# Routing inside the attentions: rows scattered to their experts, results scattered to token order, plain loads elsewhere

## What is computed

```python
logits = flat @ gate_w + gate_b                      # flat: layernorm of x, [4096, 128]
topv, topi = lax.top_k(logits, TOP_K)                # TOP_K = 2 of E = 8
topw = jax.nn.softmax(topv.astype(jnp.float32), axis=-1).astype(x.dtype)
routing = jnp.zeros_like(logits).at[jnp.arange(T)[:, None], topi].set(topw)
def body(acc, params):
    W1e, b1e, W2e, b2e, we = params
    h = jax.nn.gelu(flat @ W1e + b1e, approximate=False)
    out = h @ W2e + b2e
    return (acc + out * we[:, None], None)
...
x = x + attention_a(layernorm(x));  x = x + experts(layernorm(x))
x = x + attention_b(layernorm(x));  x = x + experts(layernorm(x))
```

## Time and profile before

| | |
|---|---|
| median of 3 runs | 1292.41 us (1289.14 to 1292.47) |
| the profiled execution, its own time | 1287.89 us |
| its span, first to last instruction | 1284.0 us |
| busy share of the span | PE 83%, DVE 63%, ACT 51%, POOL 67% |
| mean granted clock of TensorE | 0.898 of full speed |

### The profile page before, as it was taken

How to read it: one execution, slowest core, us unless ns; L and a number is a source line. 1 busy time by engine, 2 the same in 40 slices (tenths; PEclk the granted TensorE clock), 3 DMA queues, 4 the chain that set the end, 5 groups by cost and what they waited for, 6 DMA issues and landing times.

```text
span 1284.0 us, 31775 instructions
## 1 busy us (share of the span) xinstructions
PE 1068.1 (83%) x11367; PEld 807.3 (63%) x11368; DVE 811.3 (63%) x2010; ACT 650.4 (51%) x1205; POOL 865.6 (67%) x1161
## 2 busy tenths in 40 slices
PE   4699999999999757999978799999998488999200
PEld 3466676677666445999944466666665358999200
DVE  5788787788776384556426767777664754655222
ACT  1376676676766301555514567777774104555000
POOL 0599989989988256555154789998762375553576
PEclk8799999999999957999986899999998678999655
DMA  5400000000000101223310000000000002333232
GB/s 115 113 22 2 10 3 10 11 2 10 10 3 10 34 0 38 76 74 79 57 33 13 22 14 24 24 26 18 2 10 18 26 22 65 79 75 63 58 85 71
DMA packets 56248, 45.73 MB, mean 36 GB/s; under 512 B 13570, under 2 KB 48258, under 8 KB 56130
## 3 DMA queue, kind: packets, MB, share of 16 engines
q0 software_dynamic: 9088, 18.63, 6.5%
q1 hardware_dynamic: 43490, 22.46, 6.4%
q10 hardware_dynamic: 3552, 3.02, 0.9%
HBM read 27.57 MB, written 16.52 MB: 34 GB/s over the span
## 4 chain that ended last, share of the span: by engine, by line
PE 60%; DVE 13%; POOL 10%; issue 9%; ACT 4%; DMA 2%; another core or an unknown queue 2%; SPq 1%; DVEq 0%; ACTq 0%; POOLq 0%
PE PS L1778 11%; PE PS L1445 6%; PE PS L1514 5%; PE PS L1447 5%; PE PS L1565 5%; PE PS L1446 5%; POOL got L677 5%; PE PS L1496 3%; PE PS L1503 2%; PE PS L1545 2%; POOL PT L575 2%; DVE M L900 2%; PE PS L1485 1%; PE PS L1580 1%
## 5 line engine op out<-in xcount | busy, mean ns | idle before, releaser
L575 POOL TENSOR_SCALAR_AFFINE_SELECT PT<-PT 128x256 f32<-128x256 f32 x512 | 221.5, 457 | 82.4 <-ACT PT L1223 80.6
L1223 ACT ACTIVATE PT<-PS 128x768 f32<-128x768 f32 x256 | 207.1, 809 | 100.2 <-PE PS L1683 50.7
L706 POOL DMA_INDIRECT xg<-normed,source x156 | 150.9, 967 | 115.3 <-PE PS L1756 78.3
L677 POOL DMA_INDIRECT got<-expert_rows,slot_of x128 | 122.3, 956 | 79.0 <-DMA expert_rows<-y_rows 46.3
L1358 ACT ACTIVATE hid<-PS,b_cols 128x256 f32<-128x256 f32 x312 | 122.5, 476 | 102.9 <-PE PS L1447 80.0
L1778 PE MATMUL PS<-W,hid 128*128 x1248 | 155.2, 278 | 2.8 <-issue 1.8
L1778 PEld LDWEIGHTS PS<-W,hid 128*128 128x128 f32 x1248 | 148.7, 195 | 4.1 <-issue 4.1
L1514 PE MATMUL PS<-PT,v_aug 128*32 128x256 f32 (+1 forms) x2048 | 113.6, 341 | 5.4 <-POOL PT L575 5.3
L1496 PE MATMUL PS<-causal_b,ident_b 128*128 128x256 bf16 x512 | 101.9, 283 | 8.3 <-DVE q_aug L976 8.3
L1177 DVE SCALAR_TENSOR_TENSOR X<-got,weight,X 128x128 f32<-128x128 f32 x128 | 51.9, 406 | 81.1 <-DMA got<-expert_rows,slot_of 75.4
L1445 PE MATMUL PS<-xg_hi,w_hi 128*128 128x256 f32 x312 | 94.9, 304 | 3.7 <-issue 3.7
(11 more groups left out here) (264 smaller groups left out, 3227.3 us busy)
## 6 DMA issues: line engine op xcount, KB each, us to landing
expert_rows<-y_rows SPq DMA_DIRECT2D x78, 128.0 KB
normed<-xn SPq DMA_DIRECT2D x16, 256.0 KB, 2.3
xg<-normed,source POOLq DMA_INDIRECT x156
W<-in_L_ffn_w_dram SPq DMA_DIRECT2D x1, 2048.0 KB, 10.3
got<-expert_rows,slot_of POOLq DMA_INDIRECT x128
out_dram<-X SPq DMA_DIRECT2D x8, 256.0 KB
b_rows<-in_L_ffn_b_dram SPq DMA_DIRECT2D x2, 512.0 KB, 3.3
X<-in_L_attn_a_x_dram ACTq DMA_DIRECT2D x2, 256.0 KB, 4.7
```

Of the source, the lines that this page charges most:

```text
L575: ins = nc.gpsimd.affine_select(out=diagonal, in_=diagonal, pattern=[[0, 2], [1, P]], compare_op=ALU.is_ge, fill=0.0, base=0, channel_mult ...
L677: nc.gpsimd.indirect_dma_start(out=got[:, k, :], out_offset=None, in_=rows_out, in_offset=bass.IndirectOffsetOnAxis(ap=slot_of[:, which * ...
L706: nc.gpsimd.indirect_dma_start(out=xg[:, i % 4, b_, :], out_offset=None, in_=normed, in_offset=bass.IndirectOffsetOnAxis(ap=source[:, k:k ...
L1223: s.activation(PT[:, unit % 2, 2 * pair:2 * pair + 2, :], PS[:, 4:6, 0:3 * P], ACT.Exp).then_inc(m["exp_done"], 1)
```

## The change

Four things change together.

1. **Routing in the attentions.** Of the gate's logits of each chunk DVE now chooses the experts at once (`choose_first`, `choose_second`: 13 small operations on 4 blocks), PE ranks that chunk (step `rank`, 5 small matmuls), DVE adds the running count of each expert (`carry`) and writes the target row of each pair (`place`, 5 operations). For chunks 0 to 5 this rides in units 3 to 6 of the chunk two later; for chunks 6 and 7 it stands in the epilogue.
2. **Rows are scattered.** Each expert has a region of 4352 rows (STRIDE) in a DRAM tensor `expert_in`, rows of 129 numbers, the last being the place of the result. ACT writes each normalized row twice into `rows`, and POOL sends them by indirect DMAs of 128 rows (`send`), 8 for a chunk: one after each unit from unit 22 of attention a and from unit 23 of attention b, and what is left (22 and 23 of 64) after the last unit (`last_sends`). The 64 matmuls of one-hot matrices, `hot_tiles`, `block_hots`, `gather_rows`, and the stores to `normed` go.
3. **Plain loads for the tiles.** SP fills the end of each expert's last tile (8 times one register load and two DMAs), waits for all sends, and loads each tile by one DMA into `xg`. Such a load waits for `y_ready` of the tile four before (DVE now also copies the places of the results, `dest`, out of `xg`), where the gather waited for its transposes. POOL scatters each finished tile to token order by two indirect DMAs (`send_results`), where SP stored it.
4. **Plain loads for the results.** SP loads results by plain DMAs, one of 128 KB for a block of tokens after the first mixture, one of 512 KB for a chunk after the second. The 128 indirect gathers of `gather_results` go.

POOL keeps `key_low`, all of the rope, the masks and the roots. The core of the diff:

```diff
@@ the new send on POOL, and where it stands in attention_a (b the same with FIRST_SENT["b"])
+FIRST_SENT = {"a": 2 * UNITS + 6, "b": 2 * UNITS + 7}
+            def send(n, c, blocks):
+                m = att_sems[n]
+                for k in blocks:
+                    t, which = k // 2, k % 2
+                    if k == 0:
+                        pool.wait_ge(m["targets_ready"], c + 1)
+                        if c > 1:
+                            pool.wait_ge(kept[n][c % 2], 16 * 2 * CT * (c // 2))
...
+                    nc.gpsimd.indirect_dma_start(
+                        out=expert_in, out_offset=bass.IndirectOffsetOnAxis(ap=slots[:, c % 2, at:at + 1], axis=0),
+                        in_=rows[:, c % 2, t, which, :], in_offset=None).then_inc(kept[n][c % 2], 16)
+            def last_sends(n, m, which):
+                c, k = sends_at(NCH * UNITS, FIRST_SENT[n])
+                send(n, c, range(k, k + 4))
+                root(m, gate_norm_b(NCH - 1), which)
+                send(n, c, range(k + 4, 2 * CT))
+                for c in (NCH - 2, NCH - 1):
+                    send(n, c, range(2 * CT))
...
+                    if sends_at(unit, FIRST_SENT["a"]):
+                        chunk, k = sends_at(unit, FIRST_SENT["a"])
+                        send("a", chunk, range(k, k + 1))
@@ the tile's load and its fills on SP
+                sp.wait_ge(me["ends_ready"], 1)
+                    for e in range(E):
+                        end = sp.value_load(end_of[0:1, e:e + 1], min_val=0, max_val=E * STRIDE - ROWS)
+                        sp.dma_start(expert_in[bass.ds(end, ROWS), D:WIDE]...).then_inc(me["filled"], 16)
+                        sp.dma_start(expert_in[bass.ds(end, ROWS), 0:D]...).then_inc(me["filled"], 16)
...
+                def load(i, r, least):
+                    at = sp.value_load(row_of[0:1, bass.ds(i, 1)], min_val=0, max_val=E * STRIDE + SPARE - ROWS)
+                    if least >= 4:
+                        sp.wait_ge(me["y_ready"], i - 3)
+                    sp.dma_start(xg[:, r, :, :], expert_in[bass.ds(at, ROWS), :].rearrange("(b p) w -> p b w", p=P)).then_inc(me[f"row{r}"], 16)
@@ results: scattered by POOL, loaded by SP
-                        pool.wait_ge(m["turned"], i - 3)
+                    pool.wait_ge(m["y_ready"], i + 1)
...
+            for c in range(NCH):
+                sp.dma_start(result_of(c).rearrange("p t k d -> p t (k d)"), result_tiles[:, c * CT:(c + 1) * CT, :]).then_inc(results_loaded[c], 16)
@@ what is now in DVE's units of attention_a (attention_b: place at u == 6)
+                    if c > 1 and u == 3:
+                        choose_first(m, plan.find("gate", 0, c - 2))
+                    if c > 1 and u == 4:
+                        choose_second(m, c - 2)
+                    if c > 1 and u == 5:
+                        place("a", m, c - 2)
@@ ACT: the gate's rows are written twice, after the sends that last used the buffer
+                if gate and tiles[0] == 0 and c > 1:
+                    act.wait_ge(kept[n][c % 2], 16 * 2 * CT * (c // 2))
```

More of the change, by code:

```diff
@@ L1057, in experts @@
[L1057 to L1064 removed]
+                own.did(v.tensor_copy(end_of[:, :], carry[0:1, :]))
@@ L1271, in attention_a @@
                     copy_max(unit)
-                    if plan.second[unit]:
+                    if plan.second[unit] and plan.second[unit].by_act:
                         step(plan.second[unit])
```

422 lines of the change are left out of this document (208 added, 214 removed).

## The result

The changed kernel takes 1297.64 us (median of 20 runs, 1288.52 to 1307.83), the kernel before 1290.88 (20 runs). The ratio is 1.0052 (95% interval 1.0029 to 1.0075), so the change makes it slower by a little more than can be told from nothing. The forecast was 1233 us.

A forecast was written before the change was run, and what follows sets the result against it. PE was taken to bound attention a and the tiles, POOL attention b and the last stretch's gathers. Terms -49 - 17 - 16 + 27 - 4 - 2 + 2 = -59 us gave 1229, as median 1233; range 1203 to 1268.

The forecast's parts named there:

- The failed step: Attention a: DVE's added 20 operations, 4.4 us a chunk on 37.71, fit into the chunk's 53.3 us.
- The second failed step: Attention b: DVE's 4.4 us of small operations in six chunks mostly fit; 0.8 a chunk, +5 us (0 to +15).
- POOL in a: Attention a: with the sends POOL takes over as bound, 53.3 us a chunk for 47.75; +27 us, bounds +11 and +45.
- PE loses its clock: Rival, attention a: with PE busy 89% its clock falls to 0.75; +46 us, 1279; chance 0.06.
- DVE holds up the sends: Rival, attention a: every send waits for a two-input DVE operation of 0.7 us; 26 us longer, 1259; chance 0.1.
- Tiles wait for their loads: Rival, both mixtures: loads of 4.7 us make tiles 4.34 apart, 71 us, 1302; chance 0.06. The sum took +2.
- Last stretch: Last y to the end: scatters, plain loads and 64 adds of 0.405 replace gathers; -49 us, between -44 and -51.
- Up to attention b's first output: From the first mixture: scatters and plain loads give -4 us, gather waits gone early in attention b -9.
- Routing: Between each attention and its tiles: 44 us of the chain go, SP's fills end last; -17 and -16 us.

The follow-up runs named there:

- run 7: Changed kernel with attention a's choice and slots replaced by as many one-input reductions at the same places, sends to fixed rows: 1270.31 us, ratio 0.9760.
- run 1: Changed kernel without choice and rank for chunks 0 to 5 of attention a, sends staying on POOL but to fixed rows: 1253.09 us, ratio 0.9684.
- run 8: Changed kernel without choice and rank for chunks 0 to 5 of attention b, sends going to fixed rows: 1269.72 us, ratio 0.9841.
- run 9: Changed kernel with attention b's choice and slots replaced by as many one-input reductions at the same places: 1295.25 us, ratio 1.0019.
- run 10: Changed kernel with attention b's choice in four pieces, three just ahead of DVE's wait for row maxima, rank in unit 6: 1303.37 us, ratio 1.0065.
- run 3: Changed kernel with 12 matmuls on constants ahead of PE's wait for the choice in attention a: 1285.49 us, ratio 0.9936.
- run 12: Changed kernel with tile loads waiting for the fourth tile before to be turned and its places copied, not for its y: 1298.47 us, ratio 0.9993.
- run 5: Changed kernel with attention a's choice in four pieces at ends of units 3 to 6, rank starting unit 7, sends rearranged: 1300.48 us, ratio 1.0016.

## Why the prediction was wrong

**The failed step** is in "Attention a": "DVE's added 20 operations, 4.4 us a chunk on 37.71, fit into 53.3". They were priced by DVE's busy time, with the spare time of a chunk as cover. They did not fit, for two reasons. Their length was taken from a stretch where POOL was idle: 0.22 us each, against up to 2.44 us beside POOL; they added 5 to 9 us a chunk and not 4.4 (about half of their cost, run 7). And they are one link of a chain, DVE's choice, PE's rank, DVE's carry, PE's next projection, in which PE waits in order; that wait was not looked for (`rank` stands at the start of unit 5, one unit behind the choice, in the change's own plan). Leaving the choice out of a gave 45 us (run 1). Of the change's +78 in a, +41 stay without the choice (480.5 - 133.9 = 346.6 for 305.2), and 37 are the choice's.

**The second failed step** is "I take 0.8 a chunk, +5 (0 to +15)" for the same operations in attention b: leaving them out gave 28 us (run 8), outside the bounds. The reason here is mostly not POOL (run 9). What the runs show is that PE's wait for the sum `q_aug` stays with as many one-input operations (8.3 us for 7.7) and falls to 2.0 without them (run 8), so it is their number between the maxima of one unit and the sum of the next; run 10 found no better place for them.

**POOL in a:** the mechanism was right and the size somewhat low. With the sends alone most chunks take 54 to 55 us, 53.3 were forecast, and all of a is 41 us longer where 27 were forecast, within the bounds of 11 and 45; PE's waits of up to 2.9 us for `k_l` (run 1) are what a sum of busy times leaves out.

**PE loses its clock:** held at 0.06 and priced +46 by PE's busy share. The clock of PE did fall, to 0.82 to 0.94 a chunk, but by short stalls and not by the mean share: with the sends alone (run 1), PE busy 49 to 51 of 54 to 55 us, it stayed at 0.94 to 0.97 in the first four chunks that have them. Filling one of the two stalls gave 14 us in a (run 3), and b's chunks are short where the clock is full (run 10). This is a part of what the choice costs.

**DVE holds up the sends:** wrong as put; a send took 1.006 us on the mean for 0.98. It worked the other way, POOL's operations holding up DVE's.

**Tiles wait for their loads:** the third step that failed; forecast +2 for both mixtures, measured +20. The mechanism is the rival's, the size in between. The load and its hand-overs fit (2.95 us from y to the transposes, 3.3 were allowed), but of y it was said "the hand-overs some 0.1", and y came 1.0 us behind PE, 0.7 more than before the change (run 12).

**The gains** were put too small, all of them. Last stretch: -61 for -49, of which 9 are DVE's adds, 0.26 us apart (61 in 16.10 us) and not 0.405. Up to attention b's first output: -26 for -13. Routing: -21 and -20 for -17 and -16, and there SP's fills do end last, as forecast (16 of them from 543.01 to 559.7, 16.7 us for 15.0; POOL's last send starts at 551.32). The adds:

```profile
1284.06 16.10 DVE X L1216 x61
```

**The start**, +6.8, is no effect of the change: with nearly the same code up to there, 15 other kernels have their first output at 132.0 to 140.6 us, ten of them below 135.

**Slips in the sums** that change nothing: its own terms give 479.5 and not 479.1 for the first tiles (still -17), and 4.75 chunks of 5.5 us are +26 and not +27.

The range, 1203 to 1268, would have held the kernel without the choice in its units (1241), and the chance of 0.92 for faster rested on each term being independent; one shared assumption, that small operations fit into idle time, carried the two terms that failed most.

## What to carry to other kernels

Idle time of an engine covers added work only where nobody waits in order for the engine's next result; before pricing operations by the idle share, look up who reads their result next and how many instructions earlier the reader stands in its own queue. A step that hands over from one engine to another and back wants a whole unit of distance on either side: moving `rank` by less than two units, with the placing and the first send behind it, turned 0.5% slower into 1.9% faster, and run 5 shows how the same idea placed one unit wrong loses everything. Take the length of a small VectorE operation with two inputs in SBUF from a stretch where GpSimd works beside it, not from an epilogue.

## What the runs showed that I had not expected

Two stalls of TensorE, 2.65 and 1.19 us, with 1.3 us of other time between them, were followed by 6.6 us at a granted clock of 0.56; so in this stage, bound by TensorE, the stalls cost nearly twice their length (7.2 us for 3.8). Useless matmuls in the first of them made the kernel 0.9% faster (1285.49 for 1297.64 us). An operation of 0.19 us on VectorE took up to 2.44 us beside GpSimd's, longer than any one of those beside it (1.29 at most); the operations with one input kept their 0.19 us. A tile's load that waits for the result of the tile four before it made 39 tiles 3.7 us apart for 3.43, while the list of waits showed 3.2 us in the first mixture.
